# Attention block with a linear term: K of the first group ahead of the weight preparation, three weights loaded at once

## The chip, the cores and the metric

The kernel runs on one Trainium2 chip with 8 cores. Each core computes one batch element of the input on its own: the cores exchange nothing. The metric is the device time in microseconds of the slowest core. TensorE is the matmul engine (PE in the profile), VectorE is DVE, ScalarE is ACT, GpSimd is POOL, SyncE is SP. DMAs are queued by SyncE (queue q1), ScalarE (q10) and GpSimd (q0).

## What is computed

Per core, x has 4096 rows of 1024 values. The reference, cut to what matters:

```
xn = layernorm(x)
Q = xn @ W1 + b1 ; K = xn @ W2 + b2 ; V = xn @ W3 + b3
attn = softmax(Q K^T / 32)
out = x + (attn @ V) @ W4 + b4 + F(xn)
F: W_real = unfold(G1_R, G2_R), W_imag = unfold(G1_I, G2_I)   # 512 x 512 each
   out_real = xn_real @ W_real.T - xn_imag @ W_imag.T + bias_real
   out_imag = xn_real @ W_imag.T + xn_imag @ W_real.T + bias_imag
```

The kernel folds W4 into V: it computes W3' = W3 @ W4 once and uses V' = xn @ W3', so that attn @ V' needs no further product. The bias row b3 @ W4 + b4 + (bias_real, bias_imag) is likewise made once.

## The kernel before

The program is written by hand as one list of operations (`Prog`). Each engine executes its own operations in the order of the list, and waits on semaphores for the marks that an operation names. So the place of an operation in the list sets its place in its engine's queue.

The list has these parts. Names are those of the code.

- Constants: SyncE queues 23 small loads (G1, G2, b1 and b2 in eight columns each, b4, the two bias halves). b1 and b2 are loaded as 128 elements of 4 bytes per DMA. All share one semaphore, and `PRO` means that the last has landed.
- Weights: GpSimd queues W3 into `Wproj` and W4 into `W4b` (a part of KT's storage), with a cast to bf16, and b3 as a column `b3c`, 1024 elements of 2 bytes. One semaphore; `WG0` means that all three have landed. W2 is loaded into `Wproj` later (L420), once W3 has been read, and in GpSimd's queue it stands behind the normalisation of tiles 0 to 3.
- `emit_g(0)`: 8 steps, each a matmul pair into PSUM `sp_a` (L312) and an eviction by VectorE into `out2` (L319); the next step waits for the eviction. The result is written to scratch in HBM (`scw`, L323).
- 64 transposes of W3 in 32 pairs (L333, L336) into `ptA` and `ptB`, evicted by VectorE into `W3T` (L339), which lies in KT's storage too.
- `emit_g(1)`: the same for the other half. Its evictions wait for the first write to scratch.
- Read-backs: 64 DMAs on SyncE (L353), eight for each quarter of a half, and after each eight a cast by VectorE into `Wq2` (`Wqcv`, L359). `WQDONE` is the last cast.
- Layernorm of tiles 0 to 3 (128 rows each), two at a time: load on ScalarE's queue (L232, slots of two, so the load of tile n waits until tile n-2 is normalised), statistics on VectorE (L238 to L248), Ln and Exp on ScalarE, normalisation on GpSimd (L267), eight transposes on TensorE (L285, L288) in four pairs, evictions on VectorE (L291).
- The fuse W3' (L382): 8 blocks m of 16 matmuls, alternately into PSUM `po` and `pf`, evicted by ScalarE (L389).
- The bias row: 16 matmuls (L398) into `pf`, six operations on VectorE (L403 to L413) and a DMA on SyncE (L415). `CBDONE` is its landing.
- Eight groups of four tiles. Group g computes K^T (`emit_khalf`, 8 blocks of 8 matmuls of 256 columns for each half, PSUM `sp_a` and `sp_b`, evicted by ScalarE with bias b2, L430 and L440) and V' (`emit_v`, 16 matmuls per tile, PSUM `po` or `pf`, L450, evicted by ScalarE, L459), while the layernorm of the next group's four tiles runs beside it. The evictions of V' of the first 19 tiles wait for `WQDONE` and `CBDONE`, since the constants and the staging of the read-backs lie in V0's storage. The order in a group: loads and statistics of the next two tiles, K half 0, normalisation of the two, V of tiles 0 and 1, transposes of the two, then the same with K half 1, V of tiles 2 and 3.
- Then W1, and the attention over 32 row tiles, in which x is loaded and normalised once more.

Of the kernel before, what the change touches and what calls it, by code (L numbers as in the profile page):

```python
# [72 lines left out]
def build_nc(T=4096):  # L73
# [65 lines left out]
    if full:  # L139
        W3T = KT[:, 2:6, :].rearrange("p a n -> p (a n)") \  # L140
            .rearrange("p (c n) -> p c n", c=8)
    else:
        W3T = None

    if full:
        W4b = KT[:, 0:2, :].rearrange("p a n -> p (a n)") \
            .rearrange("p (c n) -> p c n", c=8)
        W3p = Ssb[:, :].bitcast(BF16).rearrange("p (c n) -> p c n", c=8)
        pro_flat = V0[:, :, :].rearrange("p a n -> p (a n)")
    else:  # L150
        W4b_t = E(nc.sbuf_tensor("W4b_t", [128, 8, D], BF16))
        W3p_t = E(nc.sbuf_tensor("W3p_t", [128, 8, D], BF16))
        W3T_t = E(nc.sbuf_tensor("W3T_t", [128, 8, D], BF16))
        pro_t = E(nc.sbuf_tensor("pro_t", [128, 19456], BF16))
        W4b = W4b_t[:, :, :]
        W3p = W3p_t[:, :, :]
        W3T = W3T_t[:, :, :]
        pro_flat = pro_t[:, :]
# [3 lines left out]
            for k in range(2)]  # L162
# [20 lines left out]
                "d_scw", "d_sra", "d_srb", "d_w10", "d_w11", "d_w12", "d_w13", "d_cbl"]  # L183
# [18 lines left out]
    for c in range(8):  # L202
# [7 lines left out]
    P.add("gpsimd", lambda e: e.dma_start(  # L210
        Wproj[:, :, :], w3_d.rearrange("(c p) n -> p c n", p=128)),
        mark=("LW3",), dma_sem="d_wg")
    P.add("gpsimd", lambda e: e.dma_start(
        W4b, w4_d.rearrange("(c p) n -> p c n", p=128)),
        mark=("LW4",), dma_sem="d_wg")
    P.add("gpsimd", lambda e: e.dma_start(
        b3c[:, :], bass.AP(b3_d.tensor, 0, [[1, 128], [128, 8]]),
        allow_slow_non_contiguous=True), mark=("Lb3c",), dma_sem="d_wg")
# [6 lines left out]
    WG0 = ("Lb3c",)  # L225
# [75 lines left out]
    def emit_ln_tile(gt, phase, extra_tp):  # L301
# [3 lines left out]
    P.add("vector", lambda e: e.tensor_copy(  # L305
        g2p[:, :, :].rearrange("p ri (g e) -> p ri g e", g=16),
        g2n[:, :, :].rearrange("p ri (e g) -> p ri g e", e=16)),
        waits=[PRO], mark=("g2perm",))

    def emit_g(ri):  # L310
        for q in range(8):
            P.add("tensor", lambda e, ri=ri, q=q: e.matmul(  # L312
                sp_a[:, 0:256], g1p[:, ri, q * 128:(q + 1) * 128],
                g2p[:, ri, :], start=True, stop=True),
                waits=[PRO, ("g2perm",),
                       ("Gev", ri, q - 1) if q > 0 else
                       (("Gev", ri - 1, 7) if ri > 0 else None)],
                mark=("Gmm", ri, q))
            P.add("vector", lambda e, ri=ri, q=q: e.tensor_copy(  # L319
                out2[:, q, :], sp_a[:, 0:256]),  # L320
                waits=[("Gmm", ri, q)] + ([("scw", 0)] if ri == 1 else []),
                mark=("Gev", ri, q))
        P.add("sync", lambda e, ri=ri: e.dma_start(  # L323
            scr_d[ri].rearrange("(q p) n -> p q n", p=128), out2[:, :, :]),
            waits=[("Gev", ri, 7)],
            mark=("scw", ri), dma_sem="d_scw")

    emit_g(0)
    for p2 in range(32):
        i, j2 = divmod(p2, 4)  # L330
        bank, bk = (ptA, "ptA") if p2 % 2 == 0 else (ptB, "ptB")
        j0 = 2 * j2
        P.add("tensor", lambda e, i=i, j0=j0, bank=bank: e.transpose(  # L333
            bank[:, 0, :], Wproj[:, i, j0 * 128:(j0 + 1) * 128], ident[:, :]),
            waits=[WG0, ("id2",), free[bk]], mark=None)
        P.add("tensor", lambda e, i=i, j0=j0, bank=bank: e.transpose(  # L336
            bank[:, 1, :], Wproj[:, i, (j0 + 1) * 128:(j0 + 2) * 128], ident[:, :]),
            mark=("w3tp", p2))
        P.add("vector", lambda e, i=i, j0=j0, bank=bank: e.tensor_copy(  # L339
            W3T[:, j0:j0 + 2, i * 128:(i + 1) * 128], bank[:, :, :]),  # L340
            waits=[("w3tp", p2)], mark=("w3te", p2))
        free[bk] = ("w3te", p2)
    emit_g(1)
    free["sp_a"] = ("Gev", 1, 7)

    for ri in range(2):
        for q in range(4):
            use = ri * 4 + q
            slot = use % 2
            dsem = "d_sra" if slot == 0 else "d_srb"  # L350
            prev = ("Wqcv", (use - 2) // 4, (use - 2) % 4) if use >= 2 else None
            for dl in range(8):
                P.add("sync", lambda e, ri=ri, q=q, dl=dl, slot=slot: e.dma_start(  # L353
                    wqst[slot][16 * dl:16 * dl + 16, :],
                    bass.AP(scr_d[ri].tensor, q * 2048 + dl * 256,
                            [[16, 16], [8192, 32], [1, 16]])),
                    waits=[("scw", ri), prev], mark=("rb", ri, q, dl),
                    dma_sem=dsem)
            P.add("vector", lambda e, ri=ri, q=q, slot=slot: e.tensor_copy(  # L359
                Wq2[:, q, ri * 512:(ri + 1) * 512], wqst[slot][:, :]),  # L360
                waits=[("rb", ri, q, 7)], mark=("Wqcv", ri, q))
    WQDONE = ("Wqcv", 1, 3)

    for u in range(2):
        emit_ln_load(u)
        emit_ln_stats(u)
    for u in range(2):
        emit_ln_apply(u)
    for u in range(2):
        emit_ln_tps(u, 1, [])  # L370
    for u in range(2, 4):
        emit_ln_load(u)
        emit_ln_stats(u)
    for u in range(2, 4):
        emit_ln_apply(u)
    for u in range(2, 4):
        emit_ln_tps(u, 1, [])
    for m in range(8):
        pv = po if m % 2 == 0 else pf
        for h in range(2):  # L380
            for k in range(8):
                P.add("tensor", lambda e, m=m, h=h, k=k, pv=pv: e.matmul(  # L382
                    pv[:, h * 512:(h + 1) * 512], W3T[:, k, m * 128:(m + 1) * 128],
                    W4b[:, k, h * 512:(h + 1) * 512],
                    start=(k == 0), stop=(k == 7)),
                    waits=[("w3te", 31), WG0,
                           ("W3pe", m - 2) if m > 1 else None],
                    mark=("W3pm", m, h) if k == 7 else None)
        P.add("scalar", lambda e, m=m, pv=pv: e.activation(  # L389
            W3p[:, m, :], pv[:, :], AF.Identity),  # L390
            waits=[("W3pm", m, 0), ("W3pm", m, 1)], mark=("W3pe", m))
    free["po"] = ("W3pe", 6)
    free["pf"] = ("W3pe", 7)
    W3PDONE = ("W3pe", 7)

    for h in range(2):
        for k in range(8):
            P.add("tensor", lambda e, h=h, k=k: e.matmul(  # L398
                pf[0:1, h * 512:(h + 1) * 512], b3c[:, k:k + 1],
                W4b[:, k, h * 512:(h + 1) * 512], start=(k == 0), stop=(k == 7)),  # L400
                waits=[WG0, free["pf"]],
                mark=("cbm", h) if k == 7 else None)
    P.add("vector", lambda e: e.tensor_copy(cbf[:, :], pf[0:1, :]),  # L403
          waits=[("cbm", 0), ("cbm", 1)], mark=("cb1",))
    P.add("vector", lambda e: e.tensor_add(cbf[:, :], cbf[:, :], b4row[:, :]),
          waits=[("cb1",), PRO], mark=("cb2",))
    P.add("vector", lambda e: e.tensor_add(cbf[:, :], cbf[:, :], cbrow[:, :]),
          waits=[("cb2",)], mark=("cb3",))
    P.add("vector", lambda e: e.tensor_copy(cbhi, cbf[:, :]),
          waits=[("cb3",)], mark=("cb4",))  # L410
    P.add("vector", lambda e: e.tensor_tensor(cbf[:, :], cbf[:, :], cbhi, ALU.subtract),
          waits=[("cb4",)], mark=("cb5",))
    P.add("vector", lambda e: e.tensor_copy(lo_stage, cbf[:, :]),  # L413
          waits=[("cb5",)], mark=("cb6",))
    P.add("sync", lambda e: e.dma_start(cbs[1:2, 0:1024], lo_stage),  # L415
          waits=[("cb6",)], mark=("cb7",), dma_sem="d_cbl")
    CBDONE = ("cb7",)
    free["pf"] = ("cb1",)

    P.add("gpsimd", lambda e: e.dma_start(  # L420
        Wproj[:, :, :], w2_d.rearrange("(c p) n -> p c n", p=128)),
        waits=[("w3tp", 31)], mark=("LW2",), dma_sem="d_wg")

    def emit_khalf(g, half):
        off = 256 * half
        for c in range(8):
            spv, spk = (sp_a, "sp_a") if c % 2 == 0 else (sp_b, "sp_b")
            for k in range(8):
# [35 lines left out]
    for g in range(NGRP):  # L464
# [5 lines left out]
        for u2 in range(2):  # L470
            emit_ln_apply(4 * (g + 1) + u2)
# [253 lines left out]
```

How the kernel before makes its waits and increments, by code:

```python
            def body(eng):  # L53
                seen = waited[engname]
                for e, fn, rw, mi in self.ops:
                    if e != engname:
                        continue
                    for semname, val in rw:
                        if seen.get(semname, -1) >= val:
                            continue
                        eng.wait_ge(sems[semname], val)
                        seen[semname] = val
                    ins = fn(eng)
                    if mi is not None:
                        semname, val, inc = mi
                        ins.then_inc(sems[semname], inc)
```

## Time and profile before

| what | us |
|---|---|
| median of 3 runs | 1732.56 |
| lowest run | 1730.74 |
| profiled execution, its time | 1731.31 |
| its span on the slowest core (core 6) | 1729.8 |
| spans of the 8 cores | 1722.0 to 1729.8 |
| TensorE busy | 1547.7 |
| VectorE busy | 755.9 |
| ScalarE busy | 482.3 |
| GpSimd busy | 128.6 |

The table gives the time of the whole program, and under it the busy time of each engine on the slowest core. The profile cuts the span into 40 equal slices of 43.2 us and gives the busy share of each engine in tenths; a digit of 9 is 90% or more. The granted clock of TensorE is given as a share of 2.4 GHz. The time of the profiled execution is 1.5 us above its span.

### The profile page before, as it was taken

The page shows a single profiled execution, that of the slowest core. Times are in us where ns is not written, and L with a number is a line of the kernel's source. Part 1 is how long each engine was busy: PE and PEld are TensorE (multiplying, and loading weights), DVE is VectorE, ACT ScalarE, POOL GpSimd, SP SyncE. Part 2 cuts the span into 40 slices and gives each one's busy share as a digit, 9 for nine tenths or more (in the row PEclk, how much of TensorE's full clock was granted, in tenths as well). Part 3 has the DMA queues.
Part 4 walks back from the last instruction along what each step waited for, and adds up shares of the span by engine and source line. Part 5 has one row for each costly group of instructions (what it writes and reads, how often), then busy time and mean ns, then how long its engine had stood idle before and what let it go on. Part 6 is the DMA issues. An engine that isn't in the chain of part 4 may idle for free.

```text
span 1729.8 us, 25401 instructions; the slowest of 8 cores (1722.0 to 1729.8 us)
## 1 busy us (share of the span) xinstructions
PE 1547.7 (89%) x8496; PEld 761.8 (44%) x8496; DVE 755.9 (44%) x1863; ACT 482.3 (28%) x873; POOL 128.6 (7%) x107
## 2 busy tenths in 40 slices
PE   0607999999899999999999999999999999999998
PEld 0203656565444444444444444444444444444443
DVE  0311433333255535553553555355535535553554
ACT  0002333343223322223222233232232232232322
POOL 0000111111100000000000000001000000000000
PEclk9999999999999999999999999999999999999999
DMA  8153211212411111101111111111011101110001
GB/s 123 45 59 71 70 54 70 74 50 74 122 37 38 37 38 49 37 37 38 49 50 37 38 37 37 37 38 49 25 49 38 59 29 38 47 37 25 25 25 37
DMA packets 69531, 83.48 MB, mean 48 GB/s; under 512 B 39699, under 2 KB 49947, under 8 KB 69406
## 3 DMA queue, kind: packets, MB, share of 16 engines
q1 hardware_dynamic: 56030, 42.01, 8.3%
q10 hardware_dynamic: 9216, 33.56, 5.8%
q0 software_dynamic: 4160, 6.29, 2.5%
q8 instruction: 72, 1.18, 0.3%
q14 instruction: 53, 0.43, 0.1%
HBM read 69.27 MB, written 18.87 MB: 51 GB/s over the span
## 4 chain that ended last, share of the span: by engine, by line
PE 89%; DVE 4%; SPq 3%; issue 2%; DMA 1%; ACT 0%; DVEq 0%; POOL 0%; ACTq 0%; POOLq 0%
PE po L648 13%; PE po L543 13%; PE po L644 13%; PE sp_a L543 6%; PE sp_b L543 6%; PE pf L573 3%; PE sp_a L430 3%; PE sp_a L510 3%; PE sp_b L510 3%; PE sp_b L430 3%; PE pf L450 3%; PE po L450 3%; PE ptA L615 2%; PE ptB L615 2%; DVE QXT L291 2%
## 5 line engine op out<-in xcount | busy, mean ns | idle before, releaser
L648 PE MATMUL po<-V,ETs 128*128 128x512 bf16 x1024 | 388.0, 379 | 0.0
L644 PE MATMUL po<-V,ETs 128*128 128x512 bf16 x1024 | 388.0, 379 | 0.0
L543 PE MATMUL po<-KT,QXT 128*128 128x512 bf16 x1024 | 231.5, 379 | 0.0
L603 DVE TENSOR_REDUCE r<-Et 128x1 f32<-128x512 bf16 x256 | 173.6, 678 | 32.0 <-ACT Et L599 31.4
L267 POOL TENSOR_SCALAR xnn<-xg,rstd,nmr 128x1024 bf16<-128x1024 f32 x64 | 76.4, 1199 | 1281.9 <-DVE nmr L263 1281.9
L599 ACT ACTIVATE Et<-Ssb,ngm 128x512 bf16<-128x512 f32 x256 | 164.6, 709 | 12.8 <-PE ptB L615 11.1
L556 ACT ACTIVATE Ssb<-sp_a 128x512 f32<-128x512 f32 x64 | 38.2, 597 | 418.9 <-DVE mx L548 227.5
L543 PEld LDWEIGHTS po<-KT,QXT 128*128 128x128 bf16 x1024 | 100.1, 98 | 120.9
L548 DVE TENSOR_REDUCE mx<-po 128x1 f32<-128x512 f32 x128 | 88.5, 692 | 131.4 <-PE po L543 131.4
L648 PEld LDWEIGHTS po<-V,ETs 128*128 128x128 bf16 x1024 | 100.0, 98 | 94.4
L644 PEld LDWEIGHTS po<-V,ETs 128*128 128x128 bf16 x1024 | 99.9, 98 | 94.5
L627 DVE COPY ETs<-ptA 128x256 bf16<-128x256 bf16 x256 | 73.4, 287 | 132.8 <-PE ptB L615 130.9
L543 PE MATMUL sp_a<-KT,QXT 128*128 128x512 bf16 x512 | 120.9, 379 | 7.7 <-ACT QXT L518 7.7
L543 PE MATMUL sp_b<-KT,QXT 128*128 128x512 bf16 x512 | 120.9, 379 | 0.0
L556 ACT ACTIVATE Ssb<-po 128x512 f32<-128x512 f32 x128 | 76.4, 597 | 143.5 <-DVE mx L548 142.1
L291 DVE COPY QXT<-ptA 128x256 bf16<-128x256 bf16 x128 | 37.3, 292 | 157.8 <-PE ptB L288 116.6
L285 PE MATMUL ptA<-ident,xnn 128*128 128x128 bf16 x128 | 28.2, 220 | 86.9 <-POOL xnn L267 51.7
L548 DVE TENSOR_REDUCE mx<-sp_a 128x1 f32<-128x512 f32 x64 | 44.1, 688 | 136.4 <-PE sp_a L543 136.4
L615 PE MATMUL ptA<-ident,Et 128*128 128x128 bf16 x512 | 70.4, 219 | 23.5 <-DVE ETs L627 13.8
L677 DVE SCALAR_TENSOR_TENSOR xr<-po,rrv,xr 128x1024 f32<-128x1024 f32 x32 | 41.1, 1284 | 94.7 <-PE po L648 94.7
L543 PEld LDWEIGHTS sp_a<-KT,QXT 128*128 128x128 bf16 x512 | 49.5, 98 | 70.0 <-issue 11.4
L615 PEld LDWEIGHTS ptA<-ident,Et 128*128 128x128 bf16 x512 | 41.5, 97 | 80.2 <-issue 48.1
(95 smaller groups left out, 1802.7 us busy)
## 6 DMA issues: line engine op xcount, KB each, us to landing
xg<-x ACTq DMA_DIRECT2D x64, 512.0 KB, 3.6
xr<-x SPq DMA_DIRECT2D x32, 512.0 KB, 3.5
out<-xr SPq DMA_DIRECT2D x32, 512.0 KB, 2.6
Wproj<-W POOLq DMA_DIRECT2D x2, 2048.0 KB, 19.3
Ssb<-W SPq DMA_DIRECT2D x8, 512.0 KB, 7.3
KT<-W POOLq DMA_DIRECT2D x1, 2048.0 KB, 32.7
scr<-V SPq DMA_DIRECT2D x2, 1024.0 KB, 4.7
V<-scr SPq DMA_DIRECT2D x64, 32.0 KB, 2.5
```

The costliest lines, as they stand in the source:

```text
L267: P.add("gpsimd", lambda e, s=s: e.tensor_scalar(xnn[:, s, :], xg[:, s, :], rstd[:, s, 0:1], nmr[:, s, 0:1], ALU.mult, ALU.add), waits=[(" ...
L430: e.matmul(spv[:, off:off + 256], Wproj[:, k, c * 128:(c + 1) * 128], xnT[:, 2 * half:2 * half + 2, k, :], start=(k == 0), stop=(k == 7)),
L450: P.add("tensor", lambda e, u=u, h=h, k=k, pv=pv: e.matmul(pv[:, h * 512:(h + 1) * 512], xnT[:, u, k, :], W3p[:, k, h * 512:(h + 1) * 512] ...
L510: P.add("tensor", lambda e, r=r, k=k, spv=spv: e.matmul(spv[:, :], Wproj[:, r, k * 128:(k + 1) * 128], xnT[:, :, k, :], start=(k == 0), st ...
L543: P.add("tensor", lambda e, tb=tb, c=c, si=si, spv=spv: e.matmul(spv, QT[:, c, si * 128:(si + 1) * 128], KT[:, c, tb * 512:(tb + 1) * 512] ...
L548: P.add("vector", lambda e, tb=tb, spv=spv: e.reduce_max(mx8[:, tb:tb + 1], spv, axis=AX.X), waits=[("Smm", i, tb)], mark=("Smx", i, tb))
L556: P.add("scalar", lambda e, tb=tb, spv=spv: e.activation(Ssb[:, tb * 512:(tb + 1) * 512], spv, AF.Identity), waits=scw_, mark=("Scp", i, tb))
L599: P.add("scalar", lambda e, tb=tb: e.activation(Et[:, tb % 4, :], Ssb[:, tb * 512:(tb + 1) * 512], AF.Exp, bias=ngm[:, 0:1], scale=SCALE), ...
L603: P.add("vector", lambda e, tb=tb: e.reduce_sum(r8[:, tb:tb + 1], Et[:, tb % 4, :], axis=AX.X), waits=[("exp", i, tb)] + ([("rr", i - 1)] ...
L615: e.transpose(bank[:, qq, :], Et[:, tb % 4, q * 128:(q + 1) * 128], ident[:, :]),
L644: P.add("tensor", lambda e, tb=tb, q=q, tj=tj: e.matmul(po[:, 0:512], ETs[:, tb % 4, q, :], V0[:, tj, 0:512], start=(tj == 0), stop=(tj == ...
L648: P.add("tensor", lambda e, tb=tb, q=q, tj=tj: e.matmul(po[:, 512:1024], ETs[:, tb % 4, q, :], V0[:, tj, 512:1024], start=(tj == 0), stop= ...
```

## The change

- The weights: GpSimd first makes the identity and the ones, then queues W2 into `Wproj`, W3 into a new place `W3B`, W4 into `W4b`, and b3c, each with a semaphore of its own. W3B, W3T and W4b lie in column ranges of KT that belong to groups 2-3, 4-5 and 6-7. The late load of W2 is gone.
- K's evictions in group 0 no longer wait for the fuse and the bias matmuls; those of groups 2 to 7 now wait for the last transpose of W3, the last eviction of the fuse, and the bias matmuls.
- The layernorm of tiles 0 to 3 and both halves of K of group 0 stand first. Behind them stands a function `emit_pro_tail`: the permutation of G2, the 32 transpose pairs of W3, G half 0, G half 1, the read-backs, the fuse, the bias row. Then V of tiles 0 and 1 and the rest of group 0.
- The fuse uses one PSUM buffer, `po`, and block m waits for the eviction of block m-1 (it was two buffers and m-2).

The diff, cut to its core (the operations in `emit_pro_tail` are those that stood in the list before, except for the lines shown):

```diff
-        W3T = KT[:, 2:6, :].rearrange("p a n -> p (a n)") \
-            .rearrange("p (c n) -> p c n", c=8)
+        W3T = KT[:, :, 2048:3072]
...
-        W4b = KT[:, 0:2, :].rearrange("p a n -> p (a n)") \
-            .rearrange("p (c n) -> p c n", c=8)
+        W3B = KT[:, :, 1024:2048]
+        W4b = KT[:, :, 3072:4096]
...
-    P.add("gpsimd", lambda e: e.dma_start(
-        Wproj[:, :, :], w3_d.rearrange("(c p) n -> p c n", p=128)),
-        mark=("LW3",), dma_sem="d_wg")
...
+    P.add("gpsimd", lambda e: e.dma_start(
+        Wproj[:, :, :], w2_d.rearrange("(c p) n -> p c n", p=128)),
+        mark=("LW2",), dma_sem="d_wg")
+    P.add("gpsimd", lambda e: e.dma_start(
+        W3B, w3_d.rearrange("(c p) n -> p c n", p=128)),
+        mark=("LW3",), dma_sem="d_wgC")
+    P.add("gpsimd", lambda e: e.dma_start(
+        W4b, w4_d.rearrange("(c p) n -> p c n", p=128)),
+        mark=("LW4",), dma_sem="d_wgB")
+    P.add("gpsimd", lambda e: e.dma_start(
+        b3c[:, :], bass.AP(b3_d.tensor, 0, [[1, 128], [128, 8]]),
+        allow_slow_non_contiguous=True), mark=("Lb3c",), dma_sem="d_wgD")
...
+    def emit_pro_tail():
...
+        for p2 in range(32):
...
+                bank[:, 0, :], W3B[:, i, j0 * 128:(j0 + 1) * 128], ident[:, :]),
+                waits=[("LW3",), ("id2",), free[bk]], mark=None)
...
+        emit_g(0)
+        emit_g(1)
...
+        for m in range(8):
+            for h in range(2):
+                for k in range(8):
+                    P.add("tensor", lambda e, m=m, h=h, k=k: e.matmul(
+                        po[:, h * 512:(h + 1) * 512], W3T[:, k, m * 128:(m + 1) * 128],
+                        W4b[:, k, h * 512:(h + 1) * 512],
+                        start=(k == 0), stop=(k == 7)),
+                        waits=[("w3te", 31), ("LW4",),
+                               ("W3pe", m - 1) if m > 0 else None],
...
-    P.add("gpsimd", lambda e: e.dma_start(
-        Wproj[:, :, :], w2_d.rearrange("(c p) n -> p c n", p=128)),
-        waits=[("w3tp", 31)], mark=("LW2",), dma_sem="d_wg")
...
-            if g == 0 and c < 6:
-                kw += [("W3pm", 7, 1), ("cbm", 1)]
+            if full and g in (2, 3):
+                kw.append(("w3tp", 31))
+            elif full and g in (4, 5):
+                kw.append(("W3pe", 7))
+            elif full and g in (6, 7):
+                kw += [("W3pe", 7), ("cbm", 1)]
...
         for u2 in range(2):
             emit_ln_apply(4 * (g + 1) + u2)
+        if g == 0:
+            emit_khalf(g, 1)
+            emit_pro_tail()
         emit_v(g, 0)
         emit_v(g, 1)
...
-        emit_khalf(g, 1)
+        if g > 0:
+            emit_khalf(g, 1)
```

## Rows read from the trace of the kernel before

**Rows 1.** The page: TensorE's busy time, then busy tenths in 40 slices.

```profile
PE 1547.7 (89%) x8496; PEld 761.8 (44%) x8496; DVE 755.9 (44%) x1863; ACT 482.3 (28%) x873; POOL 128.6 (7%) x107
PE   0607999999899999999999999999999999999998
```

**Rows 2.** Windows: length, busy us of PE, PEld, DVE, ACT, POOL; clock, DMA, GB/s.

```profile
20.00:40.00 20.00, 0.77 (x2) 0.50 (x2) 0.58 (x1) 0.00 (x0) 0.00 (x0) 1.00 0.94 122
100.00:120.00 20.00, 0.00 (x0) 0.00 (x0) 2.00 (x5) 0.00 (x0) 0.00 (x0) 1.00 0.64 61
```

**Rows 3.** Chain of waits, 0 to 200 us: start, length, engine and line.

```profile
23.86 14.55 DMA V<-bim
...
68.05 1.16 PE sp_a L312 x2
...
82.43 0.44 DVE V L319
...
83.40 0.53 SPq L353
...
118.70 2.50 DMA V<-scr
...
140.99 5.71 PE po L382 x16
146.71 3.45 PE pf L382 x16
...
183.23 3.45 PE po L450 x16
```

**Rows 4.** Chain of waits, 200 to 260 us: K's first block of group 1.

```profile
209.80 0.89 PE sp_a L430 x8
```

**Rows 5.** DMA queues by stretch (0:6, 24:30, 33:39 us): packets, MB, share.

```profile
q10 hardware_dynamic: 267, 1.02, 55.2%
...
q0 software_dynamic: 452, 0.93, 103.9%
q1 hardware_dynamic: 452, 0.00, 10.2%
...
q0 software_dynamic: 1123, 0.29, 51.0%
q1 hardware_dynamic: 450, 0.01, 11.0%
```

**Rows 6.** DMA issues, median us to landing; then Wproj's two loads, W2 and W3.

```profile
scr<-V SPq DMA_DIRECT2D x2, 1024.0 KB, 4.7
cbs<-V SPq DMA_DIRECT2D x1, 2.0 KB, 2.4
...
DMA to landing us min/median/max: 16.8/19.3/21.8
```

**Rows 7.** Timeline: start, length, instruction [idle before, and what ended it].

```profile
53.42 0.29 PE L333 MATMUL ptA<-ident,Wproj 128*128 128x128 bf16 x1
...
131.24 0.69 DVE L238 BATCH_NORM_STATS2 bn<-xg 128x6 f32<-128x512 f32 x1
...
137.31 0.27 PE L285 MATMUL ptA<-ident,xnn 128*128 128x128 bf16 x1 [6.55 <-POOL xnn L267]
...
172.15 3.61 PE L398 MATMUL pf<-KT,b3c 128*1 128x512 bf16 x16 [1.26 <-ACT Ssb L389]
...
175.87 1.21 DVE L403 COPY V<-pf 1x1024 f32<-1x1024 f32 x1 [34.48 <-PE pf L398]
...
182.67 0.62 SPq L415 DMA_DIRECT2D cbs<-V  x1
...
190.30 0.82 ACTq L232 DMA_DIRECT2D xg<-x  x2
...
194.16 0.69 DVE L238 BATCH_NORM_STATS2 bn<-xg 128x6 f32<-128x512 f32 x1 [0.76 <-DMA xg<-x]
```

**Rows 8.** Windows around the clock's fall in group 7, columns as in rows 2.

```profile
424.00:428.20 4.20, 2.90 (x23) 1.49 (x21) 1.52 (x7) 1.02 (x1) 1.14 (x1) 1.00 0.33 100
428.70:432.10 3.40, 3.40 (x19) 2.36 (x17) 2.54 (x6) 0.95 (x2) 1.49 (x1) 0.51 0.33 130
```

More of the change, by code:

```diff
@@ L150, in build_nc @@
     else:
+        W3B_t = E(nc.sbuf_tensor("W3B_t", [128, 8, D], BF16))
         W4b_t = E(nc.sbuf_tensor("W4b_t", [128, 8, D], BF16))
@@ L154, in build_nc @@
         pro_t = E(nc.sbuf_tensor("pro_t", [128, 19456], BF16))
+        W3B = W3B_t[:, :, :]
         W4b = W4b_t[:, :, :]
@@ L182, in build_nc @@
                 "d_pro", "d_wg", "d_xg0", "d_xg1", "d_xr", "d_out",
-                "d_scw", "d_sra", "d_srb", "d_w10", "d_w11", "d_w12", "d_w13", "d_cbl"]
+                "d_scw", "d_sra", "d_srb", "d_w10", "d_w11", "d_w12", "d_w13", "d_cbl", "d_wgB", "d_wgC", "d_wgD"]
     sems = {n: E(nc.semaphore(n)) for n in semnames}
@@ L208, in build_nc @@
     PRO = ("Lbi",)
-    P.add("gpsimd", lambda e: e.dma_start(
-        Wproj[:, :, :], w3_d.rearrange("(c p) n -> p c n", p=128)),
-        mark=("LW3",), dma_sem="d_wg")
-    P.add("gpsimd", lambda e: e.dma_start(
[L214 to L218, printed above, removed]
     P.add("gpsimd", lambda e: e.memset(ident[:, :], 0.0), mark=("id1",))
@@ L224, in build_nc @@
     P.add("gpsimd", lambda e: e.memset(ones1, 1.0), mark=("ones",))
-    WG0 = ("Lb3c",)
+    P.add("gpsimd", lambda e: e.dma_start(
[7 more added lines that the diff above has]
+        mark=("LW4",), dma_sem="d_wgB")
@@ L303, in emit_ln_tile @@
         emit_ln_tps(gt, phase, extra_tp)
[L305 to L420, printed above, removed]
-        Wproj[:, :, :], w2_d.rearrange("(c p) n -> p c n", p=128)),
-        waits=[("w3tp", 31)], mark=("LW2",), dma_sem="d_wg")
     def emit_khalf(g, half):
@@ L462, in emit_v @@
         free[pk] = ("Vev", g, u)
+    for u in range(2):
+        emit_ln_load(u)
+        emit_ln_stats(u)
+    for u in range(2):
+        emit_ln_apply(u)
+    for u in range(2):
+        emit_ln_tps(u, 1, [])
+    for u in range(2, 4):
+        emit_ln_load(u)
+        emit_ln_stats(u)
+    for u in range(2, 4):
+        emit_ln_apply(u)
+    for u in range(2, 4):
+        emit_ln_tps(u, 1, [])
     for g in range(NGRP):
```

81 lines of the change are left out of this document (added).

## The prediction

> **What bounds the kernel now.** I read the page first: the columns of busy time show TensorE at 89% of the span, and its slices show where the rest is [rows 1]. The reader is to see that the slices after the fourth (of 43 us each) are full, and that the holes are in the first four. So this is a kernel bound by TensorE with a slow start of some 175 us, and only the start can move. The time profiled is 1731.3 us for a span of 1729.8; the runs' median is 1732.6, 1.3 us more.
>
> Next I read the chain of waits over the start, in order of time [rows 3]. It says, in this order: the constants (queued on SyncE) land at 38.5; the 16 small G matmuls and the transposes of W3 between them end at 82.9; 64 read-backs of the G product are issued by SyncE from 83.4 and the last lands at 121.2, during which TensorE does nothing (the stretch 100 to 120 in [rows 2]); normalisation of four tiles until 140.8; the product W3·W4 from 141 to 171; the bias row; K of group 0 from 175.8; V from 183.2. From here on group follows group. The point at which everything before and after the edit can be compared is the start of K's first half of group 1: 209.80 [rows 4]. What lies behind it (1729.8 - 209.8 = 1520.0 us) is the same program on the same data in both kernels, and I take it as unchanged. So the forecast is one number: when does that K begin after the change?
>
> **The change, part by part, on one clock.**
>
> *Loads and constants.* GpSimd now queues W2, W3, W4, b3c in place of W3, W4, b3c; each weight is 2 MB written. W2 is first, so K's weights land about where W3 landed, 1.6 + 21.8 us [rows 6], 23 to 27. But K's evictions wait for the constants (PRO). What delays these today is in the view of the DMA queues by stretch [rows 5]: from 24 to 30 us GpSimd's queue q0 and SyncE's queue q1 do 452 packets each, one for one, at 75 per us, and the engines are full. Each 4-byte element of b1 and b2 waits for one 2 KB piece of a weight. Two things get worse. First, the normalisation of tiles 0 to 3 no longer stands behind the read-backs on VectorE, so x tiles 2, 3 and then 4, 5 are loaded at some 14 and 26 us, into the full engines; a pair costs 55.2% of a 6 us stretch [rows 5], 3.3 us, so 6.6 in all. Second, the last 450 packets of q1 (33 to 39 us) run today mostly beside b3c's 2-byte packets (1123 of q0 with only 0.29 MB); now they run beside W4. At 75 per us they take 6.0 us in place of 5.5, so +0.5 by the mean rate; on the slowest of the 16 engines more. The upper end is that they end with W4: one weight alone takes 16.8 us [rows 6]. I take 2.4, near the mean-rate figure. Constants: 38.5 + 6.6 + 2.4 = 47.5. Both ends for the range: 38.5 (nothing lost) and 38.5 + 6.6 + 16.8 = 61.9.
>
> *K of group 0, both halves, now first.* Tiles 0 to 3 are ready at about 29 (load landed 6 to 7, then the chain of two pairs, each about 9 us from first statistics to last transpose (131.24 to 140.8, [rows 3, 7]), with a contended load between). Two of the 16 groups of 8 matmuls fit into sp_a and sp_b; the other 14 wait for the first eviction, 0.6 us after the constants. 14 x 0.875 [rows 4] = 12.25. TensorE has stood idle before; the fuse's first group of 16 took 5.71 where the next took 3.45 [rows 3], so +2.3 for the matmuls at the lower clock level. End: 47.5 + 0.6 + 12.25 + 2.3 = 62.6. W3, needed next, is the second weight in the queue: today's second is done before 38.5, plus 6.6 is 45: in time.
>
> *W3's transposes* (32 pairs, VectorE evicting, same code): 53.42 to 68.05 [rows 3, 7] = 14.6. End 77.2.
>
> *G, both halves, now back to back.* One half takes 68.05 to 82.9 = 14.9 (eight steps of 1.87). Half 0 ends at 92.1. Half 1 reuses out2 and waits for the write to scratch, 4.7 us [rows 6]; before, the transposes hid that write. Its first eviction is at 96.9, its last matmul ends 13.0 later, at 109.9.
>
> *The read-backs.* 64 issues on SyncE, unchanged: from 83.40 to a landing at 121.2 [rows 3], 37.8. They now start at 110.5 and end at 148.3, all beside the fuse. The VectorE work queued behind their casts (the bias chain, then the evictions of the transposes of tiles 4, 5) is not wanted before 152, so 38 us of idle TensorE come off the path. This is the gain. The cover is the fuse plus the bias matmuls, and is only about 4 us longer than the read-backs.
>
> *The fuse, one PSUM buffer instead of two.* After each of m = 0..6 TensorE waits for the eviction on ScalarE. That wait has a row: the bias matmuls waited 1.26 us for the same buffer after the last one (the row at 172.15 in [rows 7]). 5.71 + 7 x (1.26 + 3.45) = 38.7, against 30 today. End 148.6. Bias matmuls 3.6: 152.2.
>
> *What is late next.* Today K's first half covers the bias row's chain; K has gone from here. The chain on VectorE starts 175.87, its DMA is issued at 182.67 and lands 2.4 later [rows 6, 7]: 9.3 us after the matmuls, so 161.4. V of tiles 0 and 1 runs 152.2 to 159.1, but their evictions wait for that DMA. Transposes of tiles 4, 5 take 3: 162. V of tile 2 needs po: eviction of tile 0 161.4 + 1.2 = 162.6; V of tiles 2, 3 ends 169.5. Meanwhile ScalarE's queue has the loads of tiles 6, 7 behind the late evictions: issued 163.6; data used 3.9 later (190.30 to 194.16), transposes start 6.1 after that (131.24 to 137.31), 3.5 for the eight pairs [rows 7]: 163.6 + 3.9 + 6.1 + 3.5 = 177.1. Today K's second half hid this load; uncovered it costs TensorE some 4 us.
>
> K of group 1 starts at 177.1 in place of 209.8: 32.7 us earlier. 1731.3 - 32.7 = 1698.6; the median lay up to 1.3 above the profiled time, so I say **1699 us**, -1.9%. The new waits in KT's evictions (groups 2 to 7) name work that ended long before: nothing. The extra semaphores: nothing.
>
> A rule of the Trainium skill speaks against the fuse's single buffer. The clock after the fuse began rose and stayed (5.71, then seven times 3.45); the one place in group work where it fell again was after 3 us of transposes alone: 1.00 until 428, then 0.51 [rows 8]. Here TensorE is busy 3.45 of every 4.7 us, which is nearer to the stretches that held. The page "TensorE: Matmul & The Clock Gate", section "A second HAM failure mode: psum-queue depth-cycling", says that short idles between groups in PSUM can make the clock swing between its two levels; by it the fuse could go as in the fourth rival, at 1724, while the rows give 1699. No stretch before the change has such pauses, so it stays a rival.
>
> **The rivals.**
> 1. The constants come no later than today: the x loads and W4 do not slow q1. For it: 4-byte packets cost little time (10.2% for 452). Against: the one-for-one rows. -9 us: 1690.
> 2. The G steps run at the upper clock level, since K precedes them. Sixteen pairs of matmuls of 1.16 to 1.20 us each would lose at most half, -9: 1690. Against: 14.6 us of transposes lie between, and 3 us of them sufficed at 428.
> 3. The constants end with W4: +14.4, 1713. For it: engines are not equally fast, and the last one counts.
> 4. The fuse stays at 1.2 GHz: 16 matmuls take 6.9 instead of 3.45, (6.9 - 5.7) + 7 x 3.4 = +25: 1724.
> 5. Slower than before: the read-backs on SyncE. Everything (VectorE's queue, V's evictions) stands behind them. Beyond the 4 us of cover each us of theirs costs one. The whole gain of 33 is gone once they take 37.8 + 4 + 33 = 75 us, twice today's; at 90 us the kernel would take 1747. For it: they are 64-byte pieces at 0.64 of the DMA share already [rows 2]. Against: nothing else moves data in that stretch, before or after.
>
> **How the numbers follow.** Forecast 0.64; rival 1 0.12; rival 2 0.06; rival 3 0.09; rival 4 0.07; rival 5 0.02. The likeliest one's own range is 1694 to 1705: its terms (constants 3, clock at the two restarts 2, scratch write 1, the tail 3) added roughly. The range of 8 in 10 takes in rivals 1 to 3: 1689 to 1714. The bound of 2%, about what a measurement of this kernel can tell from no change, is at 1697.9, one us below the forecast. So "faster" has rivals 1 and 2 (0.18) and a third of the forecast (0.2): 0.38. "Slower" is rival 5, 0.02. The rest, 0.60, is within 2%.
>
> **What would show it.** The first cast of constants on VectorE at 47.5 (not 38.5, nor 62); K's last group ends near 63; G's second half begins with a wait of VectorE or TensorE for scratch of 3 to 5 us; matmul groups in the fuse 4.7 us apart; casts of the read-backs ended before the first instruction of the bias chain; ScalarE's eviction of V tile 0 released by the bias DMA; K of group 1 at 177. What would make it wrong: a clock at 0.5 inside the fuse, read-backs that end after 152, or a change of length behind K of group 1.

## The result and the profile after

The changed kernel takes 1699.27 us (median of 10 runs) where the kernel before takes 1732.21 (10 runs): the ratio is 0.9798, with a 95% interval of 0.9765 to 0.9831. This ratio leaves out the executions in which a lower clock slowed some of the cores, which the two medians (their quotient is 0.981) keep in. So the gain is 1.9 to 2.0%, and the interval doesn't tell on which side of 2% it lies. The forecast was 1699. The profiled execution took 1699.06 us for a span of 1697.5 on its slowest core, core 5.

The page first, busy time and the slices. The columns are those of [rows 1].

```profile
span 1697.5 us, 25405 instructions; the slowest of 8 cores (1689.9 to 1697.5 us)
PE 1552.3 (91%) x8496; PEld 763.2 (45%) x8496; DVE 756.0 (45%) x1863; ACT 481.7 (28%) x873; POOL 128.7 (8%) x107
...
PE   1668899998999999999999999999999999999998
...
PEclk9769999999999999999999999999999999999999
```

The holes of the first four slices [rows 1] are partly filled, and nothing has moved after them. TensorE's busy time even grew by 4.6 us: some blocks now run at the lower clock that ran at full clock before, above all K's first blocks of groups 0 and 1 (1.87 and 1.71 us in the chain below, 0.89 in [rows 4]).

The chain of waits from 20 to 195 us on core 5 (start, length, engine and line) answers to [rows 3] and [rows 4]:

```profile
23.61 23.74 DMA V<-bim
47.43 0.48 ACT KT L436
...
48.05 1.87 PE sp_a L422 x8
...
76.17 1.16 PE sp_a L241 x2
...
90.98 6.40 DMA scr<-V
97.47 0.43 DVE V L248
...
110.77 6.43 PE po L299 x16
117.28 1.03 ACT Ssb L306
118.31 0.14 issue
118.45 3.63 PE po L299 x16
...
151.33 3.56 PE pf L315 x16
154.98 1.22 DVE V L320
...
161.79 1.73 DMA cbs<-V
163.82 3.84 DMA xg<-x
...
177.12 1.71 PE sp_a L422 x8
```

The read-backs, which were some 38 us of the chain before (83.4 to 121.2), are gone from it. In their place stand six things: the constants (until 47.4), K, W3's transposes, the G steps with a wait for the write to scratch between the halves, the fuse with pauses for ScalarE, and a tail of two DMAs. K of group 1 starts at 177.1; it was 209.8 [rows 4].

That one core is not typical. So I took the same instants on all 8 cores for every kernel that ran. The table gives the median over the cores, in us: K's first eviction (where b1 is still among the constants and K follows them, this is the end of the wait for constants), first matmul of the fuse, first of the bias row, first operation of the bias chain on VectorE, start of the last cast of the read-backs, start of K of group 1, and the rest of the span behind it.

```
kernel                  K evict  fuse   bias  chain  last cast  K group 1  rest
before                   173.9  138.8  168.9  172.6    119.1      206.3   1519.4
after                     47.0  109.6  148.9  152.6    150.3      174.0   1519.9
e1_g_apart                47.7  105.4  145.0  148.7    146.6      170.0   1519.8
e2_two_buffers            48.9  111.2  142.6  152.4    152.0      174.2   1520.1
e3_b1_last                34.2  100.3  139.8  143.5    140.9      164.8   1520.2
e4_k_half_back            46.3  104.1  143.8  147.5    145.0      173.9   1518.6
e5_no_stall               35.2   94.1  134.0  137.7    134.3      159.0   1519.4
e6_g_first                39.7   69.5  101.1  104.8  (GpSimd)     124.4   1518.2
e7_fuse_after_readback    47.8  152.6  192.1  195.8    151.8      217.2   1520.4
e8_b3c_before_w4          44.1  107.4  146.9  150.7    148.4      172.0   1519.6
```

The last column is the reason why one number was enough for a forecast: from K of group 1 to the end all kernels take 1518 to 1520 us. Before to after, K of group 1 moves by 32.3 us on the median core and the rest by 0.5.

### The profile page after: what moved, and what is told of

The parts are those of the page before. It is cut to its first block, busy times and chain, and to the rows that moved or that the text cites. A ratio compares the mean times of both kernels' runs of the same rounds, so it can differ in the third digit from the quotient of the medians.

```text
span 1697.5 us, 25405 instructions; the slowest of 8 cores (1689.9 to 1697.5 us)
## 1 busy us (share of the span) xinstructions
PE 1552.3 (91%) x8496; PEld 763.2 (45%) x8496; DVE 756.0 (45%) x1863; ACT 481.7 (28%) x873; POOL 128.7 (8%) x107
## 4 chain that ended last, share of the span: by engine, by line
PE 89%; DVE 4%; DMA 2%; issue 2%; SPq 1%; ACT 1%; DVEq 0%; POOL 0%; ACTq 0%; POOLq 0%
PE po L557 13%; PE po L662 13%; PE po L658 13%; PE sp_a L557 7%; PE sp_b L557 7%; PE pf L587 3%; PE sp_a L422 3%; PE sp_a L524 3%; PE sp_b L524 3%; PE sp_b L422 3%; PE pf L446 3%; PE po L446 3%; PE ptA L629 2%; PE ptB L629 2%; PE po L299 2%
## 5 line engine op out<-in xcount | busy, mean ns | idle before, releaser
L562 DVE TENSOR_REDUCE mx<-sp_a 128x1 f32<-128x512 f32 x64 | 44.1, 689 | 135.4 <-PE sp_a L557 135.4
L629 PE MATMUL ptA<-ident,Et 128*128 128x128 bf16 x512 | 70.4, 219 | 23.5 <-DVE ETs L641 13.8
L422 PE MATMUL sp_a<-QXT,Wproj 128*128 128x256 bf16 x512 | 69.4, 280 | 13.7 <-ACT KT L436 13.7
```

The costliest lines, as they stand in the source:

```text
L422: e.matmul(spv[:, off:off + 256], Wproj[:, k, c * 128:(c + 1) * 128], xnT[:, 2 * half:2 * half + 2, k, :], start=(k == 0), stop=(k == 7)),
L562: P.add("vector", lambda e, tb=tb, spv=spv: e.reduce_max(mx8[:, tb:tb + 1], spv, axis=AX.X), waits=[("Smm", i, tb)], mark=("Smx", i, tb))
L629: e.transpose(bank[:, qq, :], Et[:, tb % 4, q * 128:(q + 1) * 128], ident[:, :]),
```

## The experiments

All are edits of the changed kernel. Line numbers are those of its own text.

**The read-backs under the fuse, taken away again (e7_fuse_after_readback).** This tests the main claim.

```diff
-                        waits=[("w3te", 31), ("LW4",),
+                        waits=[("w3te", 31), ("LW4",), ("Wqcv", 1, 3),
```

> The changed kernel with one wait more: the fuse begins only behind the last cast of the read-backs. It takes away exactly the overlap that the prediction called the gain. Theory: the median core's fuse began at 109.6 and the last cast at 150.3, so everything moves back by 41 us: K of group 1 at about 215, time 1740, slower than the kernel before by 8 us (that is the price of the other parts of the change: late constants, half 1's wait for scratch, pauses in the fuse, lost covers). Rival: part of the 32 us comes from elsewhere (the normalisation and K brought ahead), then it stays below 1732.

Measured: 1742.6 us in the profiled execution, K of group 1 at 217.2 on the median core, 43.2 later than in the changed kernel. Two windows of core 5 (columns as in [rows 2]):

```profile
112.00:152.00 40.00, 0.34 (x1) 0.00 (x0) 3.41 (x8) 0.00 (x0) 0.00 (x0) 0.50 0.66 78
152.00:190.00 38.00, 28.05 (x112) 11.11 (x112) 0.43 (x1) 6.29 (x7) 0.00 (x0) 0.90 0.01 1
```

TensorE is empty for 40 us while the read-backs run, and the fuse follows. The overlap is the gain, all of it: without it K of group 1 starts 11 us later than in the kernel before (217.2 against 206.3). So its other parts cost some 11 us together. The next runs say where.

**The two halves of G apart (e1_g_apart).**

```diff
+        emit_g(0)
         for p2 in range(32):
...
-        emit_g(0)
         emit_g(1)
```

> The changed kernel with G half 0 moved ahead of W3's transposes and half 1 behind them, as before the change. My theory: the write of half 0 to scratch (6.4 us in the changed kernel, of which about 5 are a stop of TensorE) lies on the path, so hiding it behind the transposes brings the whole program forward by 4 to 5 us, less up to 1 us because the transposes then run at the lower clock: K of group 1 at about 173, time about 1695. Rival: the path at that place is not TensorE's chain but the read-backs and the bias chain behind them; then SyncE's start moves by the same amount and nothing differs, so this run alone can't tell the two; it prices the back-to-back G halves. A third theory, that the wait for scratch is hidden anyway, expects 1699.

Measured: 1696.7 us, ratio to before 0.9799 (0.9783 to 0.9815), which can't be told from the changed kernel's; the instants can. K of group 1 at 170.0 instead of 174.0, with constants 0.7 later: the back-to-back halves cost 4 to 5 us. The step of the change that looked like pure reordering took a cover away from a write of 1 MB.

**Two PSUM buffers in the fuse (e2_two_buffers).**

```diff
-                        po[:, h * 512:(h + 1) * 512], W3T[:, k, m * 128:(m + 1) * 128],
+                        (po if m % 2 == 0 else pf)[:, h * 512:(h + 1) * 512], W3T[:, k, m * 128:(m + 1) * 128],
...
-                               ("W3pe", m - 1) if m > 0 else None],
+                               ("W3pe", m - 2) if m > 1 else None],
```

> The changed kernel with the fuse back on two PSUM buffers. Theory A (the fuse is the path and the read-backs are its cover with about 2 us to spare): seven pauses of 1.26 us go from the fuse, 8.8 us, but the bias chain on VectorE stands behind the last read-back cast, which ended 2.2 us before it began; so 2.2 us are gained and no more: 1697, and the first instruction of the bias chain waits for a read-back. Theory B (read-backs don't matter): the whole 8.8, 1690. Theory C (the pauses in the fuse lower the clock): more than 8.8.

Measured: 1698.7 us, ratio 0.9809 (0.9793 to 0.9825), no difference that can be seen in the time. TensorE did save: from the fuse's first matmul to the bias row's first it took 31.4 us in place of 39.3. But here is VectorE's timeline on core 3:

```profile
154.94 0.43 DVE L290 CAST Wq<-V 128x512 bf16<-128x512 f32 x1 [3.63 <-DMA V<-scr]
155.28 1.21 DVE L321 COPY V<-pf 1x1024 f32<-1x1024 f32 x1
```

The cast of the last read-back ends in the moment in which the bias chain starts. It is so on all eight cores; in the changed kernel 2.2 us lie between the two on the median core (0.1 to 3.4 over the cores). From K's first eviction to K of group 1 it is 125.3 us, against 127.0: 1.7 of 7.9 us came through. Theory A holds. It also means that the price of the single buffer is 2 us here and not 9: the pauses lie in time that the read-backs need anyway.

**The constants (e3_b1_last).** b1 is wanted only in the second phase.

```diff
-        proload(("Lb1", c), b1s[:, c:c + 1], b1_d[c * 128:(c + 1) * 128].unsqueeze(1))
...
     PRO = ("Lbi",)
+    for c in range(8):
+        P.add("sync", lambda e, c=c: e.dma_start(
+            b1s[:, c:c + 1], b1_d[c * 128:(c + 1) * 128].unsqueeze(1)),
+            mark=("Lb1", c), dma_sem="d_b1")
...
-            qevw = [("Qmm", g, r), PRO]
+            qevw = [("Qmm", g, r), PRO, ("Lb1", 7)]
```

> The changed kernel with the eight loads of b1 (1024 elements of 4 bytes) behind the other constants and with a semaphore of their own. Theory (the constants are late because each small packet of SyncE's queue takes a turn with a 2 KB packet of the weights): 1090 of some 2590 packets no longer stand before the constants, about 68 turns on each of 16 engines, so they land near 27 to 30 in place of 47.4; K's first block is ready at 31, so K runs from 31 without a stop, and everything behind comes forward by about 15 us: 1684. Rival (the constants are late because a queue's last DMA completes only when the engines are no longer full, or because of the x loads alone): they land at 40 or later, gain at most 7 us: 1692 or more. Second rival: W3 lands after K ends (47) and takes part of the gain back.

Measured: 1690.8 us, ratio 0.9767 (0.9752 to 0.9781). K's first eviction is at 34.2 on the median core, 12.8 us earlier, and is now released by TensorE and no longer by the constants. So the turns of the queues were the cause of the late constants: 1024 elements fewer ahead of them, and they no longer set the start of K. But K of group 1 came forward by 9.2 only. The missing part is on ScalarE; its timeline on core 4, the slowest:

```profile
43.22 0.47 ACT L439 ACTIVATE KT<-sp_b,b2s 128x256 bf16<-128x256 f32 x1 [0.40 <-PE sp_b L425]
43.59 0.19 ACT L369 ACTIVATE sd<-vep 128x1 f32<-128x1 f32 x1
43.88 0.20 ACT L373 ACTIVATE rstd<-sd 128x1 f32<-128x1 f32 x1
48.26 0.20 ACT L369 ACTIVATE sd<-vep 128x1 f32<-128x1 f32 x1 [4.18 <-DVE vep L362]
48.55 0.20 ACT L373 ACTIVATE rstd<-sd 128x1 f32<-128x1 f32 x1
48.95 0.47 ACT L439 ACTIVATE KT<-sp_a,b2s 128x256 bf16<-128x256 f32 x1 [0.19 <-issue]
```

The Ln of tile 5 waits 4.2 us for the statistics of a tile whose load lies 14.4 us in the full DMA engines, and K's evictions, which need nothing of it, stand behind it in the queue. Of the three theories written down none had this one: W3 was not the brake.

**That stop removed, with b1 last and G apart (e5_no_stall).** The new part of the edit:

```diff
+        if g == 0:
+            emit_khalf(g, 1)
         for u2 in range(2):
             emit_ln_apply(4 * (g + 1) + u2)
         if g == 0:
-            emit_khalf(g, 1)
             emit_pro_tail()
```

> Three edits on the changed kernel: b1 behind the other constants (as in e3_b1_last), G half 0 ahead of W3's transposes (as in e1_g_apart), and the Ln and Exp of tiles 4 and 5 on ScalarE moved behind K's second half. In e3_b1_last 4.5 us of the gain of the constants were lost between K's first eviction and the first transpose (19.5 us on the median core, where the changed kernel has 15.0). Theory: these are a stop of ScalarE's queue, where Ln of tile 4 waits for an x load that is slow beside the weights, with K's evictions behind it. Then with the order changed the stretch is 15 us again, and G apart gives another 4 to 5: K of group 1 at about 156 on the median core (164.8 in e3_b1_last), 1681. Rival: the stretch is long because of W3's late landing; then it stays at 19 us and the time is 1686.

Measured: 1683.5 us, ratio 0.972 (0.9701 to 0.9739); K of group 1 at 159.0, where 156 was expected. From K's first eviction to what follows K it takes 16.4 us on the median core; e3_b1_last took 19.5 and the changed kernel 15.0. So most of the stop was this queue. K itself was faster than in the changed kernel (13.8 us from its first eviction to its last matmul, 15.3 there, median of the cores). What is left stands behind K, and the trace shows it, here on core 0:

```profile
51.80 0.21 DVE L377 TENSOR_SCALAR nmr<-bn,rstd 128x1 f32<-128x1 f32 x1 [4.54 <-ACT sd L369]
52.32 0.57 DVE L237 COPY V<-V 4x512 f32<-4x512 f32 x1
53.15 0.66 PE L244 MATMUL sp_a<-V 4*128 4x256 f32 x2 [2.40 <-DVE V L237]
```

G needs the permutation of G2 (L237) on VectorE, which stands in the queue behind `nmr` of tiles 4 and 5, and `nmr` needs the Ln and Exp that the edit has put behind K's last eviction. TensorE is idle for 2.4 us there on every core: the edit took the stop out of K and put a shorter one behind it.

**The tail of the constants beside W4 (e8_b3c_before_w4).** Only the order of two DMAs on GpSimd differs.

```diff
+    P.add("gpsimd", lambda e: e.dma_start(
+        b3c[:, :], bass.AP(b3_d.tensor, 0, [[1, 128], [128, 8]]),
+        allow_slow_non_contiguous=True), mark=("Lb3c",), dma_sem="d_wgD")
     P.add("gpsimd", lambda e: e.dma_start(
         W4b, w4_d.rearrange("(c p) n -> p c n", p=128)),
         mark=("LW4",), dma_sem="d_wgB")
-    P.add("gpsimd", lambda e: e.dma_start(
-        b3c[:, :], bass.AP(b3_d.tensor, 0, [[1, 128], [128, 8]]),
-        allow_slow_non_contiguous=True), mark=("Lb3c",), dma_sem="d_wgD")
```

> The changed kernel with the b3 column (1024 elements of 2 bytes) queued before W4 in place of behind it. Theory (the last turns of SyncE's constants go beside 2 KB packets of W4, which cost 2 to 3 us more than beside b3c's): K's first eviction comes 2 to 3 us earlier, at about 44.5 on the median core in place of 47.0, and the whole program with it, 1696.5. Rival (the loads of x alone delay the constants): no difference at K's first eviction.

Measured: K's first eviction at 44.1 instead of 47.0, and K of group 1 at 172.0 instead of 174.0; 1696.7 us in the profiled execution, ratio 0.988 with an interval so wide (0.9765 to 0.9996) that the instants say more than the time. 2.9 us for the place of 1024 two-byte elements: the prediction had put 2.4 there.

**K's second half back in its place (e4_k_half_back).**

```diff
         if g == 0:
-            emit_khalf(g, 1)
             emit_pro_tail()
...
-        if g > 0:
-            emit_khalf(g, 1)
+        emit_khalf(g, 1)
```

> The changed kernel with the second half of K of group 0 back in its old place, behind V of tiles 0 and 1 and the transposes of tiles 4 and 5. Theory (the second half was the cover of the bias row's landing and of the load of tiles 6 and 7, and without it TensorE idles some 2 us and starts K of group 1 at the lower clock): the same matmuls, 7 us, now fill these holes; K of group 1 starts at about 174.8 and at the upper clock; gain about 4 us, 1695. Rival (the holes are too short to matter, or the read-backs, which start 7 us earlier too, still set the end): no difference, 1699.

Measured: 1698.0 us, ratio 0.9807 (0.9793 to 0.9822): nothing, where 4 us were expected. The cover did what was said: from V of tile 1 to K of group 1 the matmuls of K's half (6.8 us) came in and the stretch behind them shrank by 1.8, and the rest of the span by 1.3. But W3's 32 transpose pairs took 15.9 us in place of 13.6 (median of the cores). Most of this is again a wait behind VectorE. The rows of core 5, first in e4_k_half_back, then in the changed kernel:

```profile
59.53 0.19 ACT L366 ACTIVATE sd<-vep 128x1 f32<-128x1 f32 x1
60.13 0.21 DVE L374 TENSOR_SCALAR nmr<-bn,rstd 128x1 f32<-128x1 f32 x1 [14.59 <-ACT sd L366]
60.65 0.57 DVE L234 COPY V<-V 4x512 f32<-4x512 f32 x1
61.14 0.27 DVE L269 COPY KT<-ptA 128x256 bf16<-128x256 bf16 x1
61.56 0.22 PE L263 MATMUL ptA<-ident,KT 128*128 128x128 bf16 x1 [2.27 <-DVE KT L269]
```

```profile
56.27 0.21 DVE L374 TENSOR_SCALAR nmr<-bn,rstd 128x1 f32<-128x1 f32 x1 [12.04 <-ACT sd L366]
63.42 0.22 PE L263 MATMUL ptA<-ident,KT 128*128 128x128 bf16 x1 [0.43 <-DVE KT L269]
```

The evictions of the transposes (L269) stand behind `nmr` and the permutation of G2 (L234) in VectorE's queue. In the changed kernel K's second half lies between Ln and the transposes, so both are long done; with that half gone, TensorE waits 2.27 us after the first two pairs. From the first transpose to the third pair it is 2.66 us in place of 0.82, on all eight cores: 1.8 of the 2.2 us. The clock has the rest, some 0.4: two pairs at a time take 0.82 us at the upper level and 0.91 at the lower, and about two such steps were at the upper level here, eight in the changed kernel. Gains and losses of 2 to 3 us each cancel, and the larger loss comes of the queue's order and could be taken out.

**Everything together (e6_g_first).** The core of the edits: G computed first, while the weights load (own semaphore for G1 and G2, four PSUM regions, an own staging tile for each half), b1 loaded last, the fuse on two buffers, the read-back casts on GpSimd, Ln and Exp of tiles 4, 5 behind K, the loads of tiles 6, 7 ahead of the fuse.

```diff
+    gregs = [po[:, 0:256], po[:, 512:768], pf[:, 0:256], pf[:, 512:768]]
...
+            waits=[("g2perm",), ("Gev", (n - 4) // 8, (n - 4) % 8) if n > 3 else None],
...
+    for q in range(4):
+        emit_g(0, q)
+    for u in range(2):
+        emit_ln_apply(u)
+    for q in range(4, 8):
+        emit_g(0, q)
+    for u in range(2):
+        emit_ln_tps(u, 1, [])
+    for q in range(4):
+        emit_g(1, q)
+    for u in range(2, 4):
+        emit_ln_load(u)
+        emit_ln_stats(u)
+    for q in range(4, 8):
+        emit_g(1, q)
...
-                P.add("vector", lambda e, ri=ri, q=q, slot=slot: e.tensor_copy(
+                P.add("gpsimd", lambda e, ri=ri, q=q, slot=slot: e.tensor_copy(
```

> Everything that the runs point to. Both halves of G are computed at the very start, while the weights load and TensorE is idle, with a semaphore of their own for G1 and G2, four PSUM regions and an own staging tile for each half; b1 is loaded last; the read-back casts are on GpSimd; the fuse has two buffers; Ln and Exp of tiles 4, 5 stand behind K, the loads of tiles 6, 7 ahead of the fuse. Theory (what is left is TensorE's own work): K from 34 to 49, transposes to 63, fuse to 93, bias row, V and transposes to about 119, which is K of group 1: 1640 to 1645. Rival 1: the writes to scratch and the read-backs now run beside the weight loads, take turns with 2 KB packets, and end late; the read-backs need 38 us after the weights have landed (57), so 97 or later, and each us after about 98 costs one. Rival 2: G's steps on VectorE delay the layernorm of tiles 0 to 3, K begins later than 34 by as much.

Measured: 1647.1 us in the profiled execution, ratio to before 0.951 (0.9487 to 0.9533). It beats both kernels, the one before by 5% and the changed one by 3%. The page of its slowest core, and the part of its chain that was made of read-backs in the kernel before:

```profile
span 1645.6 us, 25396 instructions; the slowest of 8 cores (1640.2 to 1645.6 us)
PE 1542.4 (94%) x8496; PEld 764.3 (46%) x8496; DVE 751.4 (46%) x1855; ACT 481.8 (29%) x873; POOL 133.2 (8%) x115
PE   5899999989999999999999999999999999999998
```

```profile
16.40 13.67 DMA xg<-x
...
38.62 1.71 PE sp_a L425 x8
...
70.75 5.08 PE po L301 x16
75.83 3.45 PE pf L301 x16
```

K of group 1 starts at 124.4, where 119 was expected: K's first eviction came at 39.7 and not at 34. Rival 2 is most of this: VectorE first waits for G2 and evicts four G steps, and the first normalisation starts at 14.5 on the median core, 10.6 in the changed kernel; the x load behind it then lies 13.7 us in the full DMA engines. From there to K of group 1 it took 84.7 us, where 85 were said. In this sum the transposes are 1.4 to 1.6 us longer by the wait of e4_k_half_back, which the order of this kernel has too. Rival 1 has a row too. The DMA view from 20 to 57 us:

```profile
scr<-V SPq DMA_DIRECT2D x1, 1024.0 KB, 35.2
```

The write to scratch took 35.2 us beside the weights, against 4.7 alone [rows 6]. The last read-back was cast at 103.4 on core 0, past the 98 from which each us was to cost one, and cost nothing:

```profile
101.28 3.81 SPq L293 DMA_DIRECT2D b1s<-b  x8
103.40 0.61 POOL L288 CAST Wq<-V 128x512 bf16<-128x512 f32 x1 [3.12 <-DMA V<-scr]
111.87 0.62 SPq L335 DMA_DIRECT2D cbs<-V  x1
```

With its casts on GpSimd, the read-backs no longer stand ahead of the bias chain on VectorE. What stands behind them is the loads of b1 and the DMA of the bias row on SyncE, and SyncE was idle for 6.8 us between the two (6.4 to 13.4 over the cores).

## Why the prediction was right

Its steps were sums on one clock, so each can be laid beside the profile of core 5.

| step | said | measured |
|---|---|---|
| constants, K's first eviction | 47.5 | 47.4 |
| K of group 0 ends | 62.6 | 62.5 |
| W3's transposes end | 77.2 | 76.1 |
| G half 0 ends | 92.1 | 91.0 |
| first eviction of half 1 | 96.9 | 97.5 |
| fuse begins | 109.9 | 110.8 |
| bias matmuls begin | 148.6 | 151.3 |
| bias matmuls end | 152.2 | 154.9 |
| bias row landed | 161.4 | 163.5 |
| loads of tiles 6, 7 issued | 163.6 | 163.8 |
| K of group 1 | 177.1 | 177.1 |

**What held.** The mechanism: e7 shows that the read-backs under the fuse are the whole gain. The late constants: e3 shows the cause, the turns of the queues. Of the two terms of their price e8 measured the second (2.9 us, said 2.4). That 2.4 was called near the mean-rate figure, which is 0.5, and no row led to it, so its size is a lucky choice. The first, 6.6 us for the x loads, no run took by itself; the sum of the two, 8.9, was right. The Trainium skill's page "DMA: Bandwidth & Descriptors", section "Queues, rings and completion order", says that each engine round-robins between the queue rows it has work for, at the granularity of packets. The row here, 492 packets of q0 and 490 of q1 from 24 to 30 us in the changed kernel, agrees with equal turns; it doesn't show how many elements go in one turn:

```profile
q0 software_dynamic: 492, 1.01, 107.5%
q1 hardware_dynamic: 490, 0.00, 11.2%
```

The second wait of half 1 (e1), and the thin cover of the read-backs (2.2 us to spare, said 4; e2 shows that it is the limit), had the right mechanism.

**What was off, and cancelled.** Five terms missed by 0.7 to 2.1 us, two of them one way and three the other, and the exact hit at the end is luck.

- The write to scratch took 6.4 us on core 5, not 4.7. It was 4.4 to 5.1 on four of the eight cores and 6.0 to 6.4 on the others.
- The fuse took 40.6 us, not 38.7. Its first block took 6.43 in place of 5.71, and a pause plus a block is 1.03 + 0.14 + 3.63 + 0.08 = 4.88 us, not 4.71: I had put the spacing of unbroken blocks, 3.45, where the last matmul has to end before ScalarE may start, 3.63. The row for this was there: the bias matmuls in [rows 7] are 3.61 long.
- The transposes were 1.1 us faster, for the most part because K left them the upper clock for their first half, which I had not counted: eight steps of 0.82 us in place of 0.91.
- The bias row, from the end of its matmuls to its landing, took 8.6 us, not 9.3: its DMA landed in 1.73 us.
- The tail, from the landing of the bias row to K of group 1, took 13.6 us, not 15.7. I let the loads of tiles 6 and 7 be issued after both evictions of V; ScalarE issued them 0.2 us after the first eviction began, before the second.
- K of group 1 then ran its first blocks at 1.71 us instead of 0.875, behind transposes and an idle stretch. That cost came behind the anchor that I had called unchanged. It went unseen since the kernel before has its own fall of the clock, in group 7 [rows 8], which core 5 of the changed kernel doesn't have: the rest is 1520.4 against 1520.0 [rows 4].

**The rivals.** 1 (constants no later) and 3 (constants with W4) fell at 47.4; W4 landed at 56.2 on core 5. 2 and 4 are settled by the clock in four windows of the changed kernel, two over the transposes, one over G, one over the fuse from its second block:

```profile
62.50:68.60 6.10, 3.70 (x35) 2.07 (x32) 3.53 (x14) 0.47 (x1) 0.00 (x0) 1.00 0.00 0
68.70:76.10 7.40, 5.17 (x35) 2.20 (x33) 4.54 (x17) 0.00 (x0) 0.00 (x0) 0.50 0.01 2
76.10:110.80 34.70, 19.05 (x34) 8.06 (x34) 6.83 (x17) 0.00 (x0) 0.00 (x0) 0.50 0.14 30
117.30:151.40 34.10, 25.36 (x113) 10.53 (x114) 2.99 (x7) 7.15 (x7) 0.00 (x0) 1.00 0.62 59
```

G ran at 0.50, so K ahead of it brought nothing (rival 2). The kernel before is no better in this, although its views give 1.00 ahead of the fuse [rows 2]: its G pairs took 1.16 to 1.20 us [rows 3] and its transposes 0.27 to 0.29 [rows 7], close to what they take at 0.50 here (1.16 to 1.20 and 0.26), while at 1.00 a G pair took 0.66 (e5_no_stall at 53.15; the view of 53 to 55 us gives 1.00 there) and a transpose 0.22 (at 63.42 above). So the clock that the views give for that start can't be relied on, and the lengths have to be read. The fuse with its pauses ran at 1.00 from its second block to the end (rival 4): the swing that the Trainium skill describes in "TensorE: Matmul & The Clock Gate", section "A second HAM failure mode: psum-queue depth-cycling", did not come with pauses of 1.25 us in every 4.88. 5 (slower read-backs) was nearer than its 0.02 suggests in one sense: on core 5 they took 40.5 us, where core 6 of the kernel before took 37.8, and 2.2 us of cover were left; on core 1 it was 0.1. The fuse beside them is hardly the reason: the medians over the cores are 38.5 us before, 39.7 here, and 39.2 in e7, where nothing runs beside them.

## What to carry to other kernels

When a DMA chain that nothing computes under is brought under work, price the cover as well as the gain: here a speed-up of the covering work by 7.9 us gave 1.7. In a start where all queues are full, count packets and not bytes, put loads of single elements last unless something waits for them, and don't queue an operation that waits for another engine ahead of work that doesn't need it: on VectorE this left TensorE idle for 1.4 us (e6) to 2.4 us (e5), and on ScalarE it stopped K's evictions for up to 4.2 us (e3). And fill the time in which weights load with the work that needs no weights: e6 starts K of group 1 50 us earlier than the changed kernel, more than the 32 of the whole reordering that was studied. G's steps and its write were 34.7 us of the chain there (76.1 to 110.8), the rest is with the smaller edits, and no run moved G alone, so its share is not shown.

## What the runs showed of the hardware that was not expected

- After K had brought TensorE to 2.4 GHz, transposes alone let it fall to half within 4 to 6.3 us over the cores (on core 5 they start at 62.6, and it is 1.00 until 68.6 and 0.50 from 68.7), and the G steps, with TensorE busy 19 of 34.7 us, never raised it. A stream with pauses of 1.25 us in every 4.88 kept it up for 34 us.
- DMAs issued beside a full software queue stretch far more than their bytes say: x loads of 512 KB took 11.6 us from issue to landing (median in the stretch from 24 to 30 us) and 3.7 over the whole program; the 1 MB write to scratch took 35.2 against 4.4 to 6.4.
- The same write, with no other DMA of its core beside it, took 4.4 to 6.4 us on the cores of one execution. The cause is open; no run tried it.
